# Attention in a four-layer block: heads in pairs on two partition halves, score and maximum matmuls interleaved

## The reference, cut to what matters

```python
# layer 2 (causal)
scores = jnp.einsum('bqhd,bkhd->bhqk', Q, K) / math.sqrt(D_K)
scores = jnp.where(causal, scores, -jnp.inf)
attn = jax.nn.softmax(scores, axis=-1)
out = jnp.einsum('bhqk,bkhd->bqhd', attn, V).reshape(Bx, Sx, N_HEADS * D_K)
return out @ W_o
# layer 3 (_mha, no mask)
scores = jnp.einsum('bhqd,bhkd->bhqk', q, k) / jnp.sqrt(jnp.asarray(hd, x.dtype))
attn = jax.nn.softmax(scores, axis=-1)
o = jnp.einsum('bhqk,bhkd->bhqd', attn, v)
return o.transpose(0, 2, 1, 3).reshape(B, S, D) @ wo.T + bo
```

## Time and profile before

| what | us |
|---|---|
| median of 3 runs | 3908.71 |
| lowest and highest | 3904.9, 3912.76 |
| the profiled execution, own time | 3900.78 |
| its span in the profile | 3898.9 |
| TensorE busy over the span | 2895.4 (74%) |
| VectorE busy over the span | 2436.3 (62%) |
| ScalarE busy over the span | 1764.7 (45%) |

### The profile page before, as it was taken

The page is one execution under the profiler, slowest core; times in us unless marked ns, Lnnn a source line. Parts: engine busy times, 40 slices in busy tenths (PEclk is TensorE's granted clock), DMA queues, the critical chain, the costliest instruction groups (busy, mean ns, idle before and its releaser), DMA issues. The chain is left out here.

```text
span 3898.9 us, 82957 instructions
## 1 busy us (share of the span) xinstructions
PE 2895.4 (74%) x22031; PEld 2090.7 (54%) x22031; DVE 2436.3 (62%) x6570; ACT 1764.7 (45%) x4634; POOL 594.0 (15%) x911
## 2 busy tenths in 40 slices
PE   0444976999898688992469999868894999994061
PEld 0233563459787458991257777765452555554060
DVE  5852767238786435775667777557446777767167
ACT  5320632334353355661346666621122666672243
POOL 0000000000000586770000000000000000000773
PEclk9977968999997899996889999886556999995595
DMA  9069200100001111224865555000255555420123
GB/s 223 5 132 250 65 6 8 33 24 0 0 1 49 37 46 57 68 66 117 283 72 67 66 64 67 13 1 0 77 188 88 64 63 63 63 34 31 47 78 101
DMA packets 348796, 264.84 MB, mean 68 GB/s; under 512 B 20504, under 2 KB 331208, under 8 KB 348040
## 3 DMA queue, kind: packets, MB, share of 16 engines
q1 hardware_dynamic: 326944, 227.12, 29.0%
q0 software_dynamic: 12928, 26.70, 2.0%
q10 hardware_dynamic: 8704, 8.39, 0.7%
HBM read 145.70 MB, written 114.86 MB: 67 GB/s over the span
## 5 line engine op out<-in xcount | busy, mean ns | idle before, releaser
L2098 PE MATMUL h_ps<-h_sk,h_sq 128*128 128x256 bf16 (+1 forms) x2048 | 407.1, 267 | 113.1 <-DMA h_vb<-v_ones 95.9
L2113 PE MATMUL h_ps<-h_sq,h_sk 128*128 128x256 bf16 (+1 forms) x2048 | 393.9, 261 | 41.5 <-issue 21.2
L2030 DVE TENSOR_REDUCE h_mx<-h_ps 128x2 f32<-128x512 f32 x512 | 333.7, 684 | 114.7 <-PE h_ps L2098 96.7
L2204 ACT ACTIVATE h_pt<-h_ps 128x512 f32<-128x512 f32 x512 | 286.9, 593 | 100.1 <-PE h_ps L2113 89.7
L1446 POOL TENSOR_TENSOR idle<-idle 128x1 f32<-128x1 f32 x400 | 101.3, 253 | 1439.0 <-ACT e_row L1510 1368.4
L2098 PEld LDWEIGHTS h_ps<-h_sk,h_sq 128*128 128x128 bf16 x2048 | 174.7, 99 | 249.2 <-issue 120.3
L2201 ACT ACTIVATE h_pt<-h_ps 128x256 f32<-128x256 f32 x512 | 196.3, 383 | 115.3 <-PE h_ps L2116 113.4
L2128 PE MATMUL h_ps_o<-h_pt,h_vb 128*9 128x256 f32 (+1 forms) x4096 | 243.2, 355 | 0.9 <-ACT h_pt L2204 0.5
L2113 PEld LDWEIGHTS h_ps<-h_sq,h_sk 128*128 128x128 bf16 x2048 | 198.7, 99 | 77.8 <-issue 27.1
L1645 POOL DMA_INDIRECT results<-e_y,e_ykey x208 | 221.6, 1065 | 70.0 <-issue 67.0
L2080 POOL TENSOR_TENSOR h_mpart<-h_mrest,h_mpart 16x256 bf16<-16x256 f32 x64 | 42.3, 661 | 1242.7 <-ACT h_mpart L2230 1242.7
(11 more groups left out here) (410 smaller groups left out, 6878.9 us busy)
## 6 DMA issues: line engine op xcount, KB each, us to landing
h_sq<-q_stack SPq DMA_DIRECT2D x64, 384.0 KB
h_sk<-k_stack SPq DMA_DIRECT2D x64, 384.0 KB
sorted_rows<-pad SPq DMA_DIRECT2D x26, 520.0 KB, 10.5
e_xt<-sorted_rows SPq DMA_DIRECT2D x52, 260.0 KB, 2.8
e_got<-results SPq DMA_DIRECT2D x48, 256.0 KB, 4.6
q_stack<-p_parts SPq DMA_DIRECT2D x32, 384.0 KB, 2.6
k_stack<-p_parts SPq DMA_DIRECT2D x32, 384.0 KB, 3.3
v_ones<-p_v SPq DMA_DIRECT2D x32, 288.0 KB, 2.6
```

Source lines behind the costliest of these rows:

```text
L2030: dve.tensor_reduce(mx[:, h, :], sv, AX, ALU.max).then_inc(s["mx"].sem, 1)
L2098: ins = pe.matmul(o, sq[u][:, h, q * P:(q + 1) * P], sk[u][:, h, 0:nk], start=True, stop=not causal)
L2113: ins = pe.matmul(o[:, q0:], sk[u][:, h, t * P:(t + 1) * P], sq[u][:, h, q0:], start=True, stop=not causal)
L2204: act.activation(to, sv, ACT.Exp, scale=scale).then_inc(s["ex"].sem, 1)
```

## The change

The sixteen heads are split into even and odd ones. `sq` and `sk` become [128, 8, 256]: an even head has its 48 + 3 rows on partitions 0 to 50, an odd head on 64 to 114, the rest of each half is zero. A score matmul now contracts over one half of 64 partitions. TensorE's step issues, for position n, the first score matmul of head n of sequence b, the first maximum matmul of head n^1 (the neighbour, on the other half) of sequence b+2, then the second of each. In the causal stage all four mask matmuls (on 128 rows) follow behind these. Both waits, for the exponential and for the maximum, stand ahead of the four. `turn_sums` moves ahead of the fourth head's scores, `turn_max` behind them, and `weigh` stays at the third head but now behind both kinds. VectorE's `norm` moves behind the fourth head's maximum. Bank numbers of head 15 and the waits of heads 0, 1 and 15 are changed to fit. Loads are seven per sequence in place of four, the way back of `m_parts` is two transfers in place of one, the ones rows eight in place of four; the bytes are the same.

```diff
-                sq = [sb(f"{tag}_sq{u}", [P, NH, SEQ], BF16, stack=st) for u in range(SLOTS)]
-                sk = [sb(f"{tag}_sk{u}", [P, NH, SEQ], BF16, stack=st) for u in range(SLOTS)]
-                zrow = sb(f"{tag}_zrow", [KM - KR, NH, SEQ], BF16, stack=st)
+                sq = [sb(f"{tag}_sq{u}", [P, NH // 2, SEQ], BF16, stack=st) for u in range(SLOTS)]
+                sk = [sb(f"{tag}_sk{u}", [P, NH // 2, SEQ], BF16, stack=st) for u in range(SLOTS)]
+                zrow = sb(f"{tag}_zrow", [KM - KR, NH // 2, SEQ], BF16, stack=st)
...
+                def bank_of(h):
+
+                    return h % 3 if h < NH - 1 else 1
...
-                            sp.dma_start(sq[u][0:KR, :, :], q_stack.rearrange("h e a t -> (e a) h t")[:, :, cols]
-                                         ).then_inc(up, 16)
...
+                            for odd in range(2):
+                                rows = slice(64 * odd, 64 * odd + KR)
+                                sp.dma_start(sq[u][rows, :, :], q_stack.rearrange("(h o) e a t -> o (e a) h t", o=2)
+                                             [odd, :, :, cols]).then_inc(up, 16)
+                                sp.dma_start(sq[u][64 * odd + KR:64 * odd + KM, :, :], zrow[:, :, :]).then_inc(up, 16)
+                                sp.dma_start(sk[u][rows, :, :], k_stack.rearrange("(h o) e a t -> o (e a) h t", o=2)
+                                             [odd, :, :, cols]).then_inc(up, 16)
...
-                        def maximum(b, h):
-                            dve.wait_ge(*at("s1", b, h + 1))
-                            if h == 0:
+                        def maximum(b, n):
+                            h = n ^ 1
+                            dve.wait_ge(*at("s1", b, n + 1))
+                            if n == 0:
...
+                                    if first:
+                                        maximum(b + 2, HG * g + j)
                                     if j == 3 and g < 2 and tail:
                                         norm(b - 1, g + 2)
                                     if j == 3 and g >= 2 and body:
                                         norm(b, g - 2)
-                                    if first:
-                                        maximum(b + 2, HG * g + j)
...
+                        def max_score(u, h, q):
+                            rows = slice(64 * (h % 2), 64 * (h % 2) + 64)
...
+                            return pe.matmul(o, sq[u][rows, h // 2, q * P:(q + 1) * P], sk[u][rows, h // 2, 0:nk],
+                                             start=(q == 0 or not causal), stop=not causal, skip_group_check=causal)
...
+                                if body:
+                                    if n == 0:
+                                        pe.wait_ge(*at("min", b, 32))
+                                    pe.wait_ge(*at("ex", b, n - 2 if 1 < n < NH - 1 else (-3, 0)[n] if n < 2 else n - 1))
+                                if first:
+                                    if n == 0:
+                                        pe.wait_ge(*s["loaded"][later].now(r_later, 112))
+                                    pe.wait_ge(*at("mx", b + 2, n - 1))
+                                for k in range(TPB):
+                                    if body:
+                                        ins = score(u, n, k)
+                                        if k == TPB - 1 and not causal:
+                                            ins.then_inc(s["s2"].sem, 1)
+                                    if first:
+                                        ins = max_score(later, n ^ 1, k)
+                                        if k == TPB - 1 and not causal:
+                                            ins.then_inc(s["s1"].sem, 1)
+                                if body and causal:
+                                    score_mask(n, 0)
+                                    score_mask(n, 1).then_inc(s["s2"].sem, 1)
+                                if first and causal:
+                                    max_mask(n ^ 1, 0)
+                                    max_mask(n ^ 1, 1).then_inc(s["s1"].sem, 1)
+
                             for g in range(GROUPS):
                                 for j in range(HG):
-                                    if body:
-                                        scores(b, u, HG * g + j)
+                                    if j == 3:
+                                        if g < 2 and tail:
+                                            turn_sums(b - 1, g + 2)
+                                        if g >= 2 and body:
+                                            turn_sums(b, g - 2)
+                                    both(HG * g + j)
```

More of the change, by code:

```diff
@@ L2003, in step @@
                                 sp.wait_ge(*at("mout", b + 1, 16))
-                                sp.dma_start(sq[ahead(u, r, 1)[0]][KR:KM, :, :], m_parts).then_inc(s["min"].sem, 16)
+                                for odd in range(2):
+                                    sp.dma_start(sq[ahead(u, r, 1)[0]][64 * odd + KR:64 * odd + KM, :, :],
+                                                 m_parts.rearrange("a (h o) t -> o a h t", o=2)[odd]
+                                                 ).then_inc(s["min"].sem, 16)
                         for b in range(SLOTS):
@@ L2087, in _ @@
                         pe.wait_ge(chained, k_set)
-                        pe.wait_ge(ones_in[n_att], 16 * SLOTS)
-                        def max_scores(b, u, r, h):
-                            if h == 0:
-                                pe.wait_ge(*s["loaded"][u].now(r, 64))
-                            pe.wait_ge(*at("mx", b, h - 1))
-                            for q in range(TPB):
-                                nk = (q + 1) * P if causal else SEQ
-                                o = ps_1[:, h % 2, q * SEQ:q * SEQ + nk]
-                                ins = pe.matmul(o, sq[u][:, h, q * P:(q + 1) * P], sk[u][:, h, 0:nk],
-                                                start=True, stop=not causal)
-                                if causal:
-                                    ins = pe.matmul(o[:, q * P:nk], mskb[:, 0:P], mskb[:, P:2 * P],
-                                                    start=False, stop=True)
-                            ins.then_inc(s["s1"].sem, 1)
@@ L2105, in scores @@
-                        def scores(b, u, h):
-                            if h == 0:
-                                pe.wait_ge(*at("min", b, 16))
-                            pe.wait_ge(*at("ex", b, h - 2 if h else 0))
-                            for t in range(TPB):
-                                q0 = t * P if causal else 0
-                                o = ps_2[:, h % 3, t * SEQ:(t + 1) * SEQ]
-                                ins = pe.matmul(o[:, q0:], sk[u][:, h, t * P:(t + 1) * P], sq[u][:, h, q0:],
-                                                start=True, stop=not causal)
-                                if causal:
-                                    ins = pe.matmul(o[:, q0:q0 + P], mskb[:, 0:P], mskb[:, 2 * P:3 * P],
-                                                    start=False, stop=True)
-                            ins.then_inc(s["s2"].sem, 1)
+                        pe.wait_ge(ones_in[n_att], 2 * 16 * SLOTS)
@@ new lines, in score, with score_mask @@
+                        def score(u, h, t):
+                            rows = slice(64 * (h % 2), 64 * (h % 2) + 64)
+                            q0 = t * P if causal else 0
+                            o = ps_2[:, bank_of(h), t * SEQ:(t + 1) * SEQ]
+                            return pe.matmul(o[:, q0:], sk[u][rows, h // 2, t * P:(t + 1) * P], sq[u][rows, h // 2, q0:],
+                                             start=(t == 0 or not causal), stop=not causal, skip_group_check=causal)
+                        def score_mask(h, t):
+                            o = ps_2[:, bank_of(h), t * SEQ + t * P:t * SEQ + (t + 1) * P]
+                            return pe.matmul(o, mskb[:, 0:P], mskb[:, 2 * P:3 * P], start=False, stop=True, skip_group_check=True)
```

32 lines of the change are left out of this document (15 added, 17 removed).

## The result

The change makes the kernel slower: 4052.4 us (median of four runs, 4044.6 to 4062.4) against 3906.8 us (3901.2 to 3912.8) beside it, ratio 1.0374, 95% interval [1.034, 1.0408]. The forecast was 4042 us.

What follows compares the result with a forecast made beforehand. TensorE was taken to bound the causal slot, TensorE and VectorE in turn the plain one. Causal +116, plain +33, start -16 make +133 us: 3900.8 becomes 4034, plus 8 for the median, 4042 us; range 3925 to 4140.

Steps and rivals of the forecast that it cites:

- rival (a): Both stages: cheap switch, 0.05 to 0.10 us, order costs in both; causal +40 to +85, 3950 to 4000 us; chance 0.22.
- 4010 to 4080: Whole kernel: the span in us given to the main forecast, with chance 0.48.
- Part 1, pairing: Both stages: two halves run side by side; four matmuls take 0.22 for 0.44 us plain, 0.22 for 0.33 causal.
- two causal values: Causal pair: 0.22 us if the four weight loads go one by one, 0.165 if not; 0.22 was taken.
- Part 2, the switch: Causal masks: each change between 64 and 128 rows costs 0.16 us, two a position; position 0.76 against 0.55 us.
- The signs that I had named for this term: Causal stage: positions start about 0.76 us apart, gaps before masks and pairs, slot period near 19.7 us.
- Part 2, the waits of the causal stage: Causal slot: further waits of TensorE taken as 0.3 us, since TensorE was held far slower than VectorE.
- The round's hole: Once a round TensorE idles 2.3 to 2.4 us, read as instructions arriving; left out as their number hardly changes.
- Part 3, plain stage: Plain stage: new order leaves VectorE idle 0.96 us behind a weigh, 4.4 against 3.3 us a slot; +33 us.
- `norm` later: Plain stage: moving `norm` behind the maximum was said to cost nothing.
- the transfers: Both stages: more loads and doubled way back of the maxima cost zero, at most 0.3 us a slot.
- Part 4, the start: Start of each stage: nine memsets with half the columns end 8 us sooner, twice, -16 us.

Runs made afterwards that it cites:

- order_only: The changed kernel with all heads back on 128 rows, so the new order without halves, in both stages; 4122.8 against 3975.8 us, ratio 1.0348.
- masks64: The changed kernel with the causal mask matmuls contracted over the head's own 64 rows, which leaves out the causal mask; 4082.9 us, ratio 1.027.
- split_fill: Kernel before with plain stage on halves, old order, waits apart, one position per group computing its score matmuls twice; 3988.5 us, ratio 1.0055.

## Why the prediction was right, and where it was not

The sign came out and the time fell where I thought it likeliest; 133 forecast, 145.3 measured by parts. But two errors of opposite sign hide in that: the causal stage came 38 us below its term (+77.7 against +116), the plain stage 55 above (+88.0 against +33). Without the 56 us of the clock, which I had not foreseen, the sum would be 3900.8 + 77.7 + 32 - 20.4 + 8 = 3998 us: the upper end of rival (a), whose cheap switch and order acting in both stages are what the runs show, and outside 4010 to 4080. That the total came so close is luck; the sign is not, since the order alone made order_only 3.5% slower.

**Part 1, pairing.** Right that halves run side by side (starts 0.00 us apart), plain pitch 0.22. Of the two causal values the other one holds: 0.17, not 0.22; the four loads do not go one by one.

**Part 2, the switch.** The signs that I had named for this term did not come: positions start 0.60 us apart, not 0.76, and the causal slot is 18.8 us on average (450.6 / 24), not 19.7. This step failed in size: "I take 0.16, the only row in which the rows change." It measures 0.10 us, the value of the weigh's entry, so a position costs 0.60 and not 0.76 us. Pitch alone is then +0.04 x 16, under a microsecond a slot. The Trainium skill, "TensorEngine Tiling (Array Packing)", section "Key Properties", has the switch drain the engine. The gaps of 0.10 us at each change of rows agree, and so does their absence in order_only and masks64.

**Part 2, the waits of the causal stage.** This step failed in kind: "TensorE is far the slower engine here (...), so I take 0.3." order_only, with neither halves nor switches, lost 68.0 of the 77.7 us. The waits of both engines were joined in one chain, and 8.8 us of reductions in a slot do not make VectorE irrelevant when each has to be released by a pair. The order was priced for the plain stage by its chain, for the causal one by comparing totals; the chain should have been walked in both. The result lies in the span that rival (a) gave this stage, 40 to 85, by its switch price too.

**The round's hole** was left out because its instructions hardly change. TensorE's hole stayed (2.2 to 2.5 us before, 2.5 to 2.9 after), but a second wait of 1.1 to 2.1 us follows it in each of six rounds, for VectorE, which comes back 1.7 to 2.7 us later from its own; and the low clock behind is twice as long. The slot with it grew by 4 us, the others by 2. Equal instructions did not mean an equal hole, since the joint wait ties TensorE to VectorE's.

**Part 3, plain stage.** Right in mechanism and size as far as it went: hole 0.98 (0.96), VectorE's idle 4.2 us a slot (4.4), slot 17.12 (17.2), +32 (+33) at the upper clock level. What it lacked was a term: the granted clock, 0.86, +56 us by the estimate above. I had read 1.00 in the earlier trace rows and carried it over to a kernel in which TensorE waits far more. `norm` later and the transfers: I saw no cost; one wait of 0.7 us for the way back of the maxima is all that 540 us of the plain stage show.

**Part 4, the start.** -8 forecast, -9.1 and -11.3 measured; the gap behind a memset shrinks too (0.49 to 0.28).

**Still open.** What in the plain stage lowers the clock. Shown: it is 0.99 with the same order on full rows, 0.86 on halves, 0.99 on halves with the pairs doubled, and with the weigh ahead 1.00 on full rows and 0.92 on halves. Not explained: why split_fill fell to 0.96. No run told apart fewer streamed columns from the shape of the waits. And order_only changed several things at once; only the weigh was moved by itself, so how the rest divides between the joint wait, the turn of the sums and `norm` is open.

## What to carry to other kernels

Where two engines release each other through two banks, a long step belongs ahead of the wait, where the other engine still has work; behind it, most of the step becomes a hole (a weigh of 1.05 us, a hole of 0.98). Walk that chain for every stage, also where one engine seems far the slower. If a change makes TensorE's work shorter without making it the bound, put its clock into the sum. And before moving an issue earlier, look at what the first consumer's wait takes together.

## What was not expected of the hardware

- Going from 64 to 128 rows or back cost 0.10 us each time, less than the 0.16 us between 1 and 128 rows.
- Weight loads for two halves start within 0.01 us of each other and do not queue.
- At the lower clock level a weigh took 1.81 us in place of 1.05; a stage whose TensorE had less to do in each position lost more to that (an estimated 56 us) than the work saved (1.25 us a slot, some 35).
- The low clock behind an idle TensorE lasted about 3 us in one kernel and over 6 in the other, at the same point of the loop.
